# The last element of a graph and LSTM kernel: its norm cut into pieces, early products moved, one element scaled on GpSimd

## The reference

```python
x = layernorm(x + L0(x, adj), axis=-1)      # x: (8, 1024, 128), adj: (1024, 1024)
x = layernorm(x + L1(x, adj), axis=-1)
# L0: three graph convolutions with adj*adj, widths 256, 512, 128
# L1: two graph convolutions with adj, then for p = 1..4: windows of p nodes go through an LSTM
#     of p steps, whose last hidden state replaces every p-th node of h
```

## Time and profile before

| | us |
|---|---|
| median of 3 runs (1012.45 to 1013.11) | 1012.63 |
| the profiled execution | 1012.88 |
| its span | 1011.2 |
| PE busy | 995.4 (98%) |
| DVE busy | 560.3 (55%) |
| ACT busy | 378.2 (37%) |
| POOL busy | 19.9 (2%) |

### The profile page before, as it was taken

The page is one execution under the profiler, slowest core; times in us unless marked ns, Lnnn a source line. Parts: engine busy times, 40 slices in busy tenths (PEclk is TensorE's granted clock), DMA queues, the critical chain, the costliest instruction groups (busy, mean ns, idle before and its releaser), DMA issues.

```text
span 1011.2 us, 14383 instructions
## 1 busy us (share of the span) xinstructions
PE 995.4 (98%) x5399; PEld 868.7 (86%) x5399; DVE 560.3 (55%) x1308; ACT 378.2 (37%) x702; POOL 19.9 (2%) x22
## 2 busy tenths in 40 slices
PE   9999999999999999999999999999999999999994
PEld 7888998888988889888898889898988989898894
DVE  7342343323334233332375656777777776767987
ACT  7231111222022120131234445445454464545765
POOL 0000000000000000000000000101010010100000
PEclk9999999999999999999999999999999999999998
DMA  9200000000000000000040000000000000000001
GB/s 358 95 1 1 1 1 1 1 1 1 1 0 0 0 0 0 0 0 0 0 166 1 1 1 1 1 1 2 22 1 21 0 21 0 21 2 22 1 1 64
DMA packets 7535, 20.42 MB, mean 20 GB/s; under 512 B 960, under 2 KB 2240, under 8 KB 7488
## 3 DMA queue, kind: packets, MB, share of 16 engines
q1 hardware_dynamic: 7488, 19.81, 5.2%
HBM read 15.61 MB, written 4.19 MB: 20 GB/s over the span
## 4 chain that ended last, share of the span: by engine, by line
PE 95%; DVE 3%; ACT 1%; issue 1%; DVEq 0%; ACTq 0%
PE ps L948 23%; PE ps L646 18%; PE ps L648 18%; PE ps L647 18%; PE ps L856 9%; PE ps L1001 2%; PE ps L1021 2%; PE ps L706 2%; PE ps L686 1%; PE ps L870 1%; PE ps L1063 1%; DVE stats L1323 1%; PE ps L1095 1%; PE ps L1064 0%; PE ps L1066 0%
## 5 line engine op out<-in xcount | busy, mean ns | idle before, releaser
L1306 DVE TENSOR_TENSOR y<-ps,y 128x512 fp32r<-128x512 f32 x46 | 31.8, 691 | 174.2 <-ACT y L1176 174.2
L1176 ACT ACTIVATE y<-ps 128x512 fp32r<-128x512 f32 x46 | 27.5, 598 | 269.3 <-PE ps L648 269.2
L646 PE MATMUL ps<-adj,node 128*128 128x512 f32 x312 | 122.2, 392 | 0.1
L648 PE MATMUL ps<-adj,node 128*128 128x512 f32 x312 | 121.7, 390 | 0.0
L647 PE MATMUL ps<-adj,node 128*128 128x512 f32 x312 | 121.6, 390 | 0.0
L646 PE MATMUL ps<-adj,h 128*128 128x512 f32 x256 | 99.7, 389 | 0.0
L647 PE MATMUL ps<-adj,h 128*128 128x512 f32 x256 | 99.7, 389 | 0.0
L648 PE MATMUL ps<-adj,h 128*128 128x512 f32 x256 | 99.6, 389 | 0.0
L1309 DVE SCALAR_TENSOR_TENSOR h<-ps,h 128x512 fp32r<-128x512 f32 x112 | 76.2, 688 | 40.0 <-ACT h L1176 39.4
L856 PE MATMUL ps<-s,adj 128*128 128x256 f32 x768 | 93.7, 283 | 0.0
L856 PEld LDWEIGHTS ps<-s,adj 128*128 128x128 f32 x768 | 92.9, 192 | 0.3
(11 more groups left out here) (214 smaller groups left out, 1690.2 us busy)
## 6 DMA issues: line engine op xcount, KB each, us to landing
square<-in_adj_t SPq DMA_DIRECT2D x8, 512.0 KB, 8.9
xb<-in_x SPq DMA_DIRECT2D x8, 512.0 KB, 11.0
adj_raw<-in_adj_t SPq DMA_DIRECT2D x8, 512.0 KB, 7.5
out<-xb SPq DMA_DIRECT2D x7, 512.0 KB, 2.7
lw_raw<-in_wih_t SPq DMA_DIRECT2D x1, 1024.0 KB, 12.4
lw_raw<-in_whh_t SPq DMA_DIRECT2D x1, 768.0 KB, 11.0
w_raw<-in_w SPq DMA_DIRECT2D x1, 512.0 KB, 11.6
out<-xb SPq DMA_DIRECT2D x1, 384.0 KB, 2.9
```

The lines of the kernel that those rows point to most:

```text
L646: pe.matmul(dst, stat(HI), mov(HI), start=start, stop=False)
L648: return pe.matmul(dst, stat(LO), mov(HI), start=False, stop=stop)
L1176: nc.scalar.activation(dst, ps[:, (j * A_MM + q) % BANKS, :], func).then_inc(a_hi, 1)
L1306: nc.vector.tensor_tensor(dst, src, f32(hi), ALU.subtract).then_inc(done, 1)
```

## The change

Element 7 is summed in tiles 0 to 3, 4 to 5 and 6 to 7; its statistics are taken in tiles 0 to 1, 2 to 5 and 6 to 7. Of its scaling ScalarE does three tiles instead of two. A new item `pool_scale` has GpSimd scale the eight tiles of element 5, in place of a shift and eight ACTIVATEs:

```diff
+                elif item[0] == "pool_scale":
+                    _, t0, t1, back = item
+                    pool.wait_ge(ln_step, PAIRS * LN_STEPS + AHEAD["norm"][B] + n_norm)
+                    for t in range(t0, t1):
+                        g = norm_column(B - back) + t
+                        rows = xb[:, B - back, t, :]
+                        last = nc.gpsimd.tensor_scalar(rows, rows, mv[:, g, 0:1], newton[:, 1, g:g + 1],
+                                                       ALU.subtract, ALU.mult)
+                    last.then_inc(rows_ready(B, t0, t1, back), 1)
```

Its wait is on the count of norm steps that the list has reached there, the two-tile statistics of element 7 among them. The change also brings code by which GpSimd could make some of the sums (`pool_adds`, `adds_so_far`, a semaphore `pool_add`), with an empty list of such sums:

```diff
+        POOL_ADDS = ()
+        def pool_adds(slot, item):
+            return slot == B and item[1:] in POOL_ADDS
...
-                                pe.wait_ge(fin_add, ahead("fin", slot, turn, n_fin - 1))
+                            by_pool, by_dve = adds_so_far(slot, n_fin - 1) if n_fin > 1 else (0, 0)
+                            if by_pool:
+                                pe.wait_ge(pool_add, by_pool)
+                            if by_dve:
+                                pe.wait_ge(fin_add, ahead("fin", slot, turn, by_dve))
```

More of the change, by code:

```diff
@@ L189, in build @@
         shift_set = sem("shift_set")
+        pool_add = sem("pool_add")
         out_ready = sem("out_ready")
@@ L336, in build @@
                 step(Y, 2, 0)]
[L338 to L348, removed]
+        LAST = [step(Z, 1, 0), step(Y, 2, 1, back=2), step(X, 4, 1, back=3, held=True), step(Z, 1, 0, BANK, held=True), step(Y, 3, 0, back=2, held=True), ("fin", 0, 4, 3), step(X, 4, 2, back=3, held=True), step(Z, 2, 0, held=True), step(Y, 3, 1, back=2), ("stats", 0, 2, 3), step(Z, 2, 1), step(Y, 3, 2, back=2, held=True), step(Z, 3, 0), ("stats", 2, 3, 3), step(X, 4, 3, back=3, held=True), step(Y, 4, 0, back=2), step(Z, 3, 1), step(Y, 4, 1, back=2), step(Z, 3, 2), ("fin", 4, 8, 3), ("ahead",), step(Y, 4, 2, back=2, held=True), step(Z, 4, 0), ("ahead",), ("stats", 3, 8, 3), ("fin", 0, 4, 2), step(Y, 4, 3, back=2, held=True), step(Z, 4, 1), ("ahead",), ("fin", 4, 8, 2), ("stats", 0, 8, 2), step(Z, 4, 2), ("root2", 0, 8, 2), ("ahead",), ("fin", 0, 4, 1), ("fin", 4, 6, 1), ("busy", 3), step(Z, 4, 3, held=True), ("stats", 0, 2, 1), ("end",), ("shift", 0, 8, 2), ("pool_scale", 0, 8, 3), ("stats", 2, 6, 1), ("fin", 6, 8, 1), ("stats", 6, 8, 1), ("root", 0, 8, 1), ("shift", 5, 8, 1), ("scale", 0, 5, 1)]
+        POOL_ADDS = ()
         SLOTS = B + 1
@@ L368, in parts_of @@
         def parts_of(e):
-            return sum(not isinstance(item, Step) and item[0] in ("scale", "shift") and slot - item[3] == e
+            return sum(not isinstance(item, Step) and item[0] in ("scale", "shift", "pool_scale") and slot - item[3] == e
                        for slot, full in ((B - 1, DRAIN), (B, LAST)) for item in full)
@@ L378, in norm_column, with adds_so_far @@
             return NORM_COLUMN.get(e, 0)
+        def pool_adds(slot, item):
+            return slot == B and item[1:] in POOL_ADDS
+        def adds_so_far(slot, n_fin):
+            first = [item for item in items(slot) if item[0] == "fin"][:n_fin]
+            by_pool = sum(pool_adds(slot, item) for item in first)
+            return by_pool, n_fin - by_pool
         def items(slot):
@@ L393, in items @@
                 else:
-                    back = item[-1] if item[0] in ("fin", "stats", "root", "root2", "scale", "shift") else 0
+                    back = item[-1] if item[0] in ("fin", "stats", "root", "root2", "scale", "shift", "pool_scale") else 0
                 if slot < back:
@@ L639, in _ @@
                 last.then_inc(runs_set, 1)
+            n_fin, n_norm = 0, 0
+            for item in items(B):
+                if item[0] == "fin":
+                    _, t0, t1, back = item
+                    if pool_adds(B, item):
+                        pool.wait_ge(fin_mm, AHEAD["fin"][B] + n_fin + 1)
+                        rows = xb[:, B - back, t0:t1, :].rearrange("p t c -> p (t c)")
+                        nc.gpsimd.tensor_tensor(rows, rows, ps[:, GB + n_fin % 2, 0:(t1 - t0) * F],
+                                                ALU.add).then_inc(pool_add, 1)
+                    n_fin += 1
+                elif item[0] == "stats":
+                    n_norm += 2
+                elif item[0] in ("root", "root2"):
+                    n_norm += LN_STEPS - 2
+                elif item[0] == "pool_scale":
+                    _, t0, t1, back = item
+                    pool.wait_ge(ln_step, PAIRS * LN_STEPS + AHEAD["norm"][B] + n_norm)
[5 more added lines that the diff above has]
+                    last.then_inc(rows_ready(B, t0, t1, back), 1)
         @block.tensor
@@ L1090, in pe_slot @@
                             lo_reached(0)
-                            if n_fin > 1:
-                                pe.wait_ge(fin_add, ahead("fin", slot, turn, n_fin - 1))
+                            by_pool, by_dve = adds_so_far(slot, n_fin - 1) if n_fin > 1 else (0, 0)
[3 more added lines that the diff above has]
+                                pe.wait_ge(fin_add, ahead("fin", slot, turn, by_dve))
                         for t in range(t0, t1):
@@ L1707, in dve_slot @@
                         _, t0, t1, back = item
+                        if pool_adds(slot, item):
+                            n_fin += 1
+                            continue
                         dve.wait_ge(fin_mm, ahead("fin", slot, turn, n_fin + 1))
@@ L1721, in dve_slot @@
                         if item[0] == "stats":
-                            dve.wait_ge(fin_add, ahead("fin", slot, turn, n_fin))
+                            by_pool, by_dve = adds_so_far(slot, n_fin) if slot == B else (0, n_fin)
+                            if by_pool:
+                                dve.wait_ge(pool_add, by_pool)
+                            if by_dve or slot < B:
+                                dve.wait_ge(fin_add, ahead("fin", slot, turn, by_dve))
                             free = (out_ready, e if e == TWO_ROOTS else b + 1)
```

## The result

| | median us | runs | ratio to before, 95% interval |
|---|---|---|---|
| before | 1012.94 | 16 | |
| changed | 1014.86 | 16 | 1.0018, 1.0011 to 1.0025 |

The changed kernel is 1.9 us slower, clear of noise, where 1011.9 (1010.9 to 1014.2) was forecast. Its profiled run took 1014.28 us with a span of 1012.6. One of the sixteen runs of each kernel took over twice as long (3529 and 2719 us); the ratio is taken without them.

What follows compares the result with a forecast made beforehand. TensorE carries 95% of the chain, but the edit touches only the last slot, where VectorE's tail and the last outputs count. Terms -0.20 + 0.30 - 0.65 = -0.55, perhaps 0.1 to 0.2 more, from 1012.63: 1011.9 us, 8-in-10 range 1010.9 to 1014.2.

Steps and rivals of the forecast that it cites:

- the price of GpSimd's scaling: Element 5's scaling on GpSimd: 0.38 us an operation, ends 0.21 and 0.84, from a 128x128 select (0.29) and 128x516 casts (0.84).
- done by about 1007: Condition of the -0.65 us for outputs: GpSimd's eight operations on element 5 end by about 1007 us; about 1004.6 was expected.
- first sign of being wrong: In the profile after: a GpSimd row of over 0.5 us an operation without VectorE holding it.
- The term for the outputs: Kernel's end: both 512 KB outputs leave ahead of the last, which then lands sooner; -0.65 us, ends -0.9 and 0.
- the pieces: VectorE's tail: last element's sums and statistics in parts, five tiles scaled instead of six; 0.97 + 0.29 - 1.20 - 0.26 = -0.20 us.
- GpSimd's hold on VectorE: VectorE's tail: output product or shift and one or two root steps (0.2 each) meet GpSimd; +0.3 us, ends 0 and 3.5.
- GpSimd is slow: Rival, at the root: 0.84 us an operation, VectorE's root steps each wait for one, +3.1 us; 1015.4 us, chance 17%.
- Is done with VectorE: Last element: ScalarE scales three tiles instead of two at 0.39 us each, after the root, and ends with VectorE.
- The early products and fillers: Z(4,2)'s input products run before transposes, fillers 0 and 3: gates up to 1.5 us sooner, VectorE no sooner; value 0.
- Statistics beside GpSimd: Statistics on VectorE while GpSimd scales element 5: priced like the sum from PSUM, unhindered.
- the second rival: Before the root, statistics and GpSimd alternate, 8 x 0.38 = 3.0 us lost, less 0.3 already counted; 1014.6 us, chance 5%.
- The third rival: GpSimd's first use costs 6 us more, element 5's output leaves at about 1010.5, the last ones behind it; 1015.5 us, 4%.

Runs made afterwards that it cites:

- e8: Kernel before plus seven groups of three GpSimd operations on spare tiles at about 205 us, to price the scaling; 0.79 us at 128 columns.
- e2: Changed kernel with SyncE issuing element 6's output before element 5's; 1013.51 us.
- e7: Changed kernel with element 5 split at the same place: tiles 0 to 3 scaled on GpSimd, 4 to 7 on ScalarE; 1011.95 us.
- e11: Changed kernel with element 5 split at the same place: six tiles scaled on GpSimd, two on ScalarE; 1013.24 us.
- e3: Changed kernel with GpSimd's scaling released right after the root of elements 5 and 6 instead of after the two-tile statistics; 1012.50 us.
- e9: Changed kernel with four tiles of element 5 on GpSimd right after the root, four on ScalarE, shifts ahead of the two-tile statistics; 1011.74 us.
- e10: Kernel before with only the scaling of element 5, all eight tiles, moved to GpSimd, released by the root of elements 5 and 6; 1012.60 us.
- e12: As e9, with the transfer of ScalarE's last three tiles issued by ScalarE itself instead of SyncE; 1011.75 us.
- e1: Changed kernel with element 5 scaled on ScalarE again, everything else as changed; 1013.84 us.
- e5: Kernel before with only element 7's sums and statistics in pieces, five tiles on VectorE, three on ScalarE; element 5 on ScalarE; 1013.63 us.
- e6: Kernel before with only early products ahead of transposes, fewer fillers, and element 5's statistics ahead of a sum; 1012.69 us, ratio 1.0000.

## Why the prediction was wrong

**The failed step: the price of GpSimd's scaling, "I take 0.38, nearest to the select", and with it the condition "It needs GpSimd's eight operations to be done by about 1007."** They take 0.79 (6.35 us for eight in the timeline after; alone in e8 too). It is also the first sign of being wrong that the prediction names: a GpSimd row of over 0.5 us. The ends I gave, 0.21 and 0.84, hold it; the choice was wrong. I chose by the shape of the output, 128x128, when what matters is what is done to each element. The cast, 0.84 for 516 columns, was no upper end in kind either; that it lies close is chance.

**What followed from it.** The term for the outputs, -0.65, became +1.81. I had the mechanism (what stands in front of the last transfer at 400 GB/s) and its condition, and lost its sign with the price: 6.35 us from 1000.39 is 1006.74, half a microsecond before VectorE's last scaling ends. (The output product, which I let hold GpSimd off for 0.5 us, did not: GpSimd starts inside it, and its first operation takes 0.90.) "Done by about 1007" was too weak a condition besides: elements 5 and 6 together need 2.6 us of queue, so they have to be out some 2.6 us before the last pieces. e2, e7 and e11 show that.

In one sum, against the kernel before, counted from the mark: the pieces gave -0.59 where I had -0.20, GpSimd's hold on VectorE +0.85 where I had +0.30, the outputs +1.81 where I had -0.65; together +2.07 where I had -0.55. The outputs make 2.46 of the 2.62 us between the two.

Even with GpSimd in time the term -0.65 was too large for this order of work. From VectorE's last scaling to the end of the span it was 3.55 us before, 3.50 in e3, 3.38 in e7 and 3.17 in e9: 0.05 to 0.38 won. The last transfer does land sooner (after 2.3 to 2.6 us instead of 2.9), but it is issued 0.43 to 0.47 us after VectorE's last scaling instead of 0.17, because ScalarE's third tile makes its piece ready at the same time and SyncE issues that one first; I had allowed 0.05 for it. In e10, where ScalarE scales two tiles, the issue comes 0.03 after the scaling and the 0.70 of the term are there. e12 takes that wait away and wins nothing, since both transfers then share the rate.

**The rival that came true, and how far.** "GpSimd is slow" gave 1015.4 at 0.84, and 1014.86 was measured, but its 3.1 us for VectorE were 0.85 (11.90 against e1's 11.05; the root alone is 0.80 longer). I had read the 0.85 us of a root step beside a cast as "a step waits for the whole operation". Beside the scaling five of the nine steps take 0.25 to 0.38 instead of 0.17, and four are not held at all. The nearness of 1015.4 is two errors against each other: too much for the port, and for the queue -0.1 in place of +1.81.

**The root steps.** +0.3 was expected, 0.85 came, since the root met GpSimd all the way and not for one or two steps. The price of one meeting, 0.2, came out near: 0.08 to 0.21 each. That is luck, since a meeting that lasts the whole of an operation would have cost more with one of 0.79.

**The pieces.** -0.20 was forecast, -0.59 measured (e1, e5). By terms, read in e5: the two sums ahead of the cell +0.94 (forecast +0.97); statistics between cell and output product +0.12 (+0.29: the first operations of the statistics start in the last cell operation's shadow, and the next one in theirs); output product to root -1.40 (-1.20); five tiles instead of six -0.25 (-0.26). The waits at each piece that I allowed for hardly show.

**ScalarE.** "Is done with VectorE" was right in the changed kernel (1007.12 and 1007.24). What the GpSimd edit buys was mis-told, though: e1 and e5 show that the pieces alone make ScalarE last by 1.8 us, so the relief was worth more to them than the place in the queue alone: e7, in which ScalarE has fifteen scalings instead of e1's nineteen, is 1.55 us under e1 (-0.70 against +0.85).

**The early products and fillers**: value 0, right (e6). The gates of Z(4,2) came 1.5 us sooner and VectorE turned to them when it had turned to them before. The clock stayed at 1.00 (994 to 996 us above) through TensorE's idle time of 1.2 us before the last products, as taken from the earlier trace rows.

**Statistics beside GpSimd**: no row of before had them, and I priced them as unhindered. With GpSimd running one takes 0.28 us (at 1002.46 above), as without it (0.29 and less). For the statistics the trace thus agrees with the rule of "SBUF — State Buffer" in the Trainium skill, section "Who interferes with whom", that a VectorE instruction with at most one SBUF input, outside its two-port modes, does not contend with GpSimd; the second rival falls. The same section says of a VectorE instruction in a two-port mode that, where GpSimd was first, it is fully blocked for the whole of GpSimd's instruction. The trace does not name the modes. Beside a cast of 0.84 a root step took 0.85; beside a scaling of 0.79 the two root steps with one input (1003.05 and 1003.34) took 0.25 and 0.32 instead of 0.17. If they were in such a mode, the measurement differs from the page for this operation. The third rival, a first use that costs 6 us, falls too: GpSimd's first scaling starts at 1000.39, 0.10 after the statistics it waits for.

What stays open is why a meeting costs 0.2 and not 0.79. The rows would fit an operation that holds the port only for its passage over the tile (a copy is 0.29); this is a guess, and none of the runs measures it.

## What to carry to other kernels

Price an operation on an engine by what it does to each element, not by the shape of its tile alone: where no row has it and the ends are a factor of four apart, forecast with the upper end too, and ask which deadline each end meets. At a kernel's end, outputs that leave in program order share one rate, so the deadline of all but the last is its start less their bytes over that rate (2.6 us for 1 MB here). A piece moved to a slow engine belongs at the first moment at which its inputs exist, and only as much of it as ends in time. Eight tiles at the late place lost 1.9 us; eight at the root won 0.5 (e3), four at the late place 0.7 (e7), and four at the root, with the shifts for ScalarE moved forward as well, 1.2 (e9). Of the three gains only the last is clear of noise against the kernel before.

## What the runs showed of the hardware

- GpSimd's scaling with two column scalars: 0.79, 0.58, 0.47 us at 128, 64, 32 columns; with constants 0.64; one operation with one column scalar 0.60; a product of two tiles 0.40; a copy 0.29 (e8). A product of two tiles is cheaper than one scaling.
- A VectorE root step beside that scaling is held up 0.08 to 0.21 us, or not at all; beside a 516-wide cast 0.68 (0.85 against 0.17).
- GpSimd is held up as well: one scaling beside VectorE's cell took 1.30 us instead of 0.79 (e9, from 999.00), while the cell's last two operations took 0.42 and 0.48 (0.42 and 0.43 in e1, without GpSimd). With four tiles the early place thus costs GpSimd time, and VectorE next to nothing (tail 11.10 against 11.05 in e1).
- SyncE's issue of a transfer took 0.34 to 0.50 us, the last two together 0.82 to 0.88, in before, e1, e3, e7 and e9; with more output still in front of them the last two took 1.19 (e11), 1.26 (e2) and 2.02 us (the changed kernel).
